# A macaron block on one core: from stages over both batch rows to one batch row beside the other's expert matmuls

## The chip, the cores and the metric

The kernel runs on one core of one Trainium2 chip, launched once. The metric is the device time of that core in microseconds (us); the median of three runs stands for a kernel. PE is TensorE, DVE VectorE, ACT ScalarE, POOL GpSimd, and SP the sync engine, which only issues DMAs here.

## The reference

`x` has 2 batch rows of 2048 tokens with 128 features, all in fp32. Three residual parts follow one another:

```python
x = x + 0.5 * ffn(layernorm(x))     # 4 experts, each token goes to one of them
x = x + attn(layernorm(x))          # linear attention with 32 features
x = x + 0.5 * ffn(layernorm(x))     # the same expert weights again

def ffn(x):                         # W1: 4 x 128 x 512, W2: 4 x 512 x 128
    idx = argmax(softmax(x @ Wg + bg))
    y = gelu(x @ W1 + b1) @ W2 + b2     # for every expert
    return y[idx]
def attn(x):
    q1, k1 = (elu(p) + 1 for p in (x @ Wq.T @ proj, x @ Wk.T @ proj))
    kv = k1.T @ (x @ Wv.T)              # summed over the 2048 tokens of a batch row
    return (q1 @ kv) / (sum(q1) + 1e-8)
```

Only the sum `kv` joins tokens, and only those of one batch row. Everything else is done for each token alone.

## The kernel before

The kernel works on both batch rows together, in stages that follow one another:

1. **Front.** `x` is loaded as 32 tiles of 128 tokens. DVE makes the layer norm, PE transposes and multiplies by `Wg`, and rows of `x` and of its norm are stored to a buffer in DRAM (`rows0`).
2. **Routing** (`route_dve`, `route_pe`). DVE finds each token's expert and, with two small matmuls, its place in an order by expert. Each expert gets whole tiles of its own, so 32 tiles become T1 = 35, with empty slots at an expert's end. A one-hot matrix `SL` and the table `AV` turn this into a list `src` of the rows of each tile.
3. **Experts** (`ffn_pool`, `ffn_pe`, `ffn_act`, `ffn_dve`), 35 tiles. POOL gathers a tile by an indirect DMA (L548); PE transposes it (L595), multiplies by W1 (`up`, L602) and, after ACT's GELU (L644), by W2 (`down`, L612). DVE copies the expert's W1 and bias into `w1e` (L666), adds residual and bias (L675) and the result of `down` (L686). The buffers `g_in`, `w1e`, `res` have U = 4 copies.
4. **Attention**, over all 35 tiles in groups of 5: `la_*` makes features and the sums, `lb_*` (L823, L832 to L844) the result and the statistics of the next layer norm. Two-row masks keep the batch rows apart. Rows go to `rows1`.
5. **Routing** again, 6. **Experts** again, now with a scatter of each tile to the output (L556), by the token number that the row carries.

Each engine runs a program of its own in the order in which its block is written, and waits on semaphores; `run_steps` and `run_groups` write loops with a peeled head and tail. Nothing is reordered at run time. So no matmul of an expert stage can be issued while PE's program stands in attention or routing. An fp32 matmul counts as two instructions in the profile, a transpose as one: a tile has 8 for `up`, 8 for `down` and 1 for the transpose.

Of the kernel before, what the change touches and what calls it, by code (L numbers as in the profile page):

```python
# [5 lines left out]
class Step:  # L15

    def __init__(self, j, k, turns16, bufs):
        self.j, self.k, self.turns16, self.bufs = j, k, turns16, bufs  # L20

    def plus(self, d):
        k = self.k + d
        return Step(self.j + d, k % self.bufs, self.turns16 + 16 * (k // self.bufs), self.bufs)

    def at_most(self, last):
        return not isinstance(self.j, int) or self.j <= last


def step_of(j, bufs):  # L30
    return Step(j, j % bufs, 16 * (j // bufs), bufs)


def run_steps(eng, head, loop_end, n, bufs, body, enter=None, after_loop=None):

    assert head % bufs == 0 and (loop_end - head) % bufs == 0
    shared = None
    for j in range(head):  # L40
        if enter and j % bufs == 0:
            shared = enter(j)
        body(step_of(j, bufs), shared)
    with eng.Fori(head, loop_end - bufs + 1, bufs) as i:
        shared = enter(i) if enter else None
        for u in range(bufs):
            body(Step(i + u, u, i * (16 // bufs), bufs), shared)
    if after_loop:
        after_loop()
    for j in range(loop_end, n):  # L50
        if enter and j % bufs == 0:
            shared = enter(j)
        body(step_of(j, bufs), shared)


def run_groups(eng, n, parts, before=None):


    most = max(lag for lag, _ in parts)
    loops = (n - 3) // 2  # L60

    def peeled(s):
        if before:
            before(s)
        for lag, body in parts:
            if 0 <= s - lag < n:
                body(step_of(s - lag, 2))
    for s in range(3):
        peeled(s)
    if before:  # L70
        before(3)
    with eng.Fori(3, 2 + 2 * loops, 2) as i:
        for u in range(2):

            st = Step(i + u, (1 + u) % 2, (i - 1) * 8 + 16 * ((1 + u) // 2), 2)
            for lag, body in parts:
                body(st.plus(-lag))
    for s in range(3 + 2 * loops, n + most):
        for lag, body in parts:
            if 0 <= s - lag < n:  # L80
                body(step_of(s - lag, 2))


class Stage:


    AHEAD = 2
# [8 lines left out]
def need(eng, stage, j):  # L96

    if isinstance(j, int) and j < 0:
        return
    eng.wait_ge(stage.sem, j + 1 + Stage.AHEAD)  # L100


def build(nc, x, wq, wk, wv, proj, w1, b1, w2, b2, wg, bg, out):
# [5 lines left out]
    TOKENS = B * L  # L109
# [3 lines left out]
    T0 = TOKENS // P  # L113
    T1 = T0 + NE - 1
    GS0, GS1 = 4, 5
    NG0, NG1 = T0 // GS0, T1 // GS1
    U = 4
    EW = F + NC
    WG = 96
    EPS_LN, EPS_Z = 1e-5, 1e-8  # L120
    FAR = 2 * TOKENS
    BANK = 512
    assert D == P and T1 % GS1 == 0 and T0 % GS0 == 0 and B == 2 and B * R <= P

    x_rows = x.rearrange("b l d -> (b l) d").rearrange("(p t) d -> p t d", t=T0)
    out_rows = out.rearrange("b l d -> (b l) d")


    RW0, RW1 = 2 * D, 2 * D + 1
    rows0 = nc.dram_tensor("rows0", (TOKENS, RW0), f32, kind="Internal").ap()  # L130
    rows1 = nc.dram_tensor("rows1", (P * T1 + 1, RW1), f32, kind="Internal").ap()
    rows0_v = rows0.rearrange("(p t) c -> p t c", t=T0)
    rows1_v = rows1[0:P * T1, :].rearrange("(p t) c -> p t c", t=T1)

    with ExitStack() as ctx:
# [3 lines left out]
        def pair(name, shape, dt=f32, n=2):  # L139
            return [sb(f"{name}{i}", shape, dt) for i in range(n)]  # L140
# [961 lines left out]
```

## Time and profile before

| | us |
|---|---|
| median of 3 runs | 353.05 |
| the runs | 349.28 to 356.53 |
| span of the profiled execution (no other time of it is given) | 349.7 |
| PE busy | 248.7 (71%) |
| DVE busy | 174.6 (50%) |
| POOL busy | 145.9 (42%) |
| ACT busy | 136.8 (39%) |

The span is the time from the first to the last instruction. "Busy" is the union of an engine's instructions; for PE it also holds time in which matmuls overlap. A stage is found in the trace by its lines: PE's first `up` starts at 56.15 us, its last instruction of the first expert stage ends near 128, routing lies around 205 to 223, the second expert stage from 228 to 338.

### The profile page before, as it was taken

To read this page: it belongs to the slowest core of one execution; us is meant where nothing else is said; L and a number is where in the kernel's file an instruction comes from. 1 tells how busy PE (TensorE), PEld (TensorE's weight loads), DVE (VectorE), ACT (ScalarE), POOL (GpSimd) and SP (SyncE) were. 2 spreads that over 40 slices of the span, in tenths; PEclk is the share of its full clock that TensorE was granted. 3 is DMA by queue.
4 is the path that set the end of the run, shared out by engine and by line. 5 is a ranking of instruction groups with operands and counts; after the bars stand their busy time and mean duration, and the time that the engine had idled before them with its cause. 6 is when DMAs were issued, how large, how long until landed. Compare 5 with 4: busy or idle time off the path is not lost. (4 is left out here: it accounts for less than half of the span.)

```text
span 349.7 us, 7231 instructions
## 1 busy us (share of the span) xinstructions
PE 248.7 (71%) x1825; PEld 232.3 (66%) x1826; DVE 174.6 (50%) x791; ACT 136.8 (39%) x436; POOL 145.9 (42%) x172
## 2 busy tenths in 40 slices
PE   0577036999999997997699640669687776876740
PEld 0566026999999996986599540659676765875740
DVE  3965882456555578836655249723232333233320
ACT  0133003666667634551644420036441543353520
POOL 2710216354454264220523202256557555765650
PEclk9999655999999999998555665599789889889995
DMA  6946503122222203222593400031212212212200
GB/s 248 301 126 195 148 2 90 50 73 69 66 60 62 59 2 148 83 72 74 153 184 100 114 0 0 13 95 55 61 54 68 60 53 60 68 53 60 51 26 0
DMA packets 27941, 28.45 MB, mean 81 GB/s; under 512 B 2938, under 2 KB 23052, under 8 KB 27666
## 3 DMA queue, kind: packets, MB, share of 16 engines
q1 hardware_dynamic: 20274, 14.57, 14.7%
q0 software_dynamic: 4480, 11.30, 11.6%
q10 hardware_dynamic: 3168, 2.36, 2.3%
q8 instruction: 8, 0.13, 0.1%
q14 instruction: 11, 0.09, 0.1%
HBM read 13.87 MB, written 11.09 MB: 71 GB/s over the span
## 5 line engine op out<-in xcount | busy, mean ns | idle before, releaser
L644 ACT ACTIVATE hT<-PA,w1e 128x128 f32<-128x128 f32 x280 | 80.0, 371 | 65.9 <-PE PA L602 32.3
L602 PE MATMUL PA<-hT_in,w1e 128*128 128x128 f32 x560 | 83.3, 296 | 21.6 <-DVE w1e L666 10.7
L548 POOL DMA_INDIRECT g_in<-rows,g_idx x70 | 68.6, 980 | 59.5 <-issue 21.2
L602 PEld LDWEIGHTS PA<-hT_in,w1e 128*128 128x128 f32 x560 | 75.2, 209 | 24.5 <-ACT hT_in L638 20.9
L612 PE MATMUL PC<-W,hT 128*128 x560 | 78.1, 286 | 0.2 <-issue 0.2
L612 PEld LDWEIGHTS PC<-W,hT 128*128 128x128 f32 x560 | 72.5, 203 | 0.4 <-issue 0.3
L556 POOL DMA_INDIRECT out_dram<-o_out,o_idx x35 | 36.6, 1046 | 33.1 <-issue 16.1
L638 ACT ACTIVATE hT_in<-PD 128x128 f32<-128x128 f32 x70 | 20.4, 292 | 64.6 <-PE PD L595 57.6
L685 DVE COPY o_idx<-token 128x1 int32<-128x1 int32 x35 | 5.3, 153 | 72.1 <-PE PC L612 50.1
L666 DVE COPY w1e<-W 128x516 f32 x72 | 29.9, 422 | 0.9 <-DVE W L974 0.8
L595 PE MATMUL PD<-ident,g_in 128*128 128x128 f32 x70 | 21.4, 306 | 11.1 <-DMA g_in<-rows,g_idx 10.7
L353 PE MATMUL PA<-ident,xn 128*128 128x128 f32 x102 | 19.1, 327 | 10.1 <-DVE xn L343 3.6
L686 DVE SCALAR_TENSOR_TENSOR X<-PC,res 128x128 f32 (+1 forms) x35 | 10.2, 292 | 30.3 <-PE PC L612 26.3
L366 PE MATMUL PB<-Wg,xnT 128*128 128x96 f32 x134 | 23.0, 337 | 0.0
L854 ACT ACTIVATE xn<-X,nmr,rstd 128x128 f32 (+1 forms) x35 | 14.2, 481 | 21.8 <-POOL nmr L816 21.0
L1003 PE MATMUL PB<-ident 128*128 128x128 f32 x72 | 13.0, 360 | 13.5 <-DVE STATS L957 12.2
L353 PEld LDWEIGHTS PA<-ident,xn 128*128 128x128 f32 x102 | 14.2, 173 | 12.6 <-issue 12.6
L366 PEld LDWEIGHTS PB<-Wg,xnT 128*128 128x128 f32 x134 | 22.4, 255 | 0.2 <-ACT xnT L360 0.2
L322 POOL TENSOR_TENSOR MR<-VE,neghalf 128x4 f32<-128x4 f32 (+1 forms) x15 | 16.0, 1108 | 14.3 <-DVE VE L313 14.2
L343 DVE TENSOR_SCALAR xn<-X,mr 128x128 f32 (+1 forms) x67 | 19.2, 350 | 5.2 <-DMA rows<-xn 2.1
L360 ACT ACTIVATE xnT<-PA 128x640 f32<-128x640 f32 (+1 forms) x22 | 14.5, 661 | 17.8 <-PE PA L353 17.8
L520 PE MATMUL PC<-AV,SL 128*128 128x70 bf16 x67 | 5.7, 249 | 21.9 <-DVE SL L464 21.9
(148 smaller groups left out, 286.5 us busy)
## 6 DMA issues: line engine op xcount, KB each, us to landing
rows<-X SPq DMA_DIRECT2D x7, 322.5 KB, 4.0
XN<-xn SPq DMA_DIRECT2D x7, 320.0 KB, 2.5
rows<-xn SPq DMA_DIRECT2D x7, 320.0 KB, 4.6
X<-in_L_attn_x_dram SPq DMA_DIRECT2D x2, 1024.0 KB, 6.5
rows<-xn SPq DMA_DIRECT2D x8, 256.0 KB, 2.3
rows<-X SPq DMA_DIRECT2D x1, 2048.0 KB, 9.5
g_in<-rows,g_idx POOLq DMA_INDIRECT x70
qs<-QT SPq DMA_DIRECT2D x7, 160.0 KB, 2.6
```

The costliest lines, as they stand in the source:

```text
L322: eng.tensor_tensor(MR[:, g * gs:(g + 1) * gs, 1], VE[:, g * gs:(g + 1) * gs], neghalf[:, 0:gs], ALU.pow)\
L343: i = eng.tensor_scalar(xn[k][:, t, :], row(X, st.j * gs + t), mr[k][:, t, 0:1], mr[k][:, t, 1:2], ALU.subtract, ALU.mult)
L353: i = eng.transpose(area[:, t * P:(t + 1) * P], xn[st.k][:, t, :], ident[:, :])
L366: i = eng.matmul(PB[:, BANK * st.k + t * WG:BANK * st.k + (t + 1) * WG], xnT[st.k][:, t * P:(t + 1) * P], Wg[:, :], start=True, stop=True)
L548: eng.indirect_dma_start(out=g_in[k][:, 0:RW], out_offset=None, in_=rows, in_offset=bass.IndirectOffsetOnAxis(ap=g_idx[k][:, 0:1], axis=0))\
L556: eng.indirect_dma_start(out=out_rows, out_offset=bass.IndirectOffsetOnAxis(ap=o_idx[k][:, 0:1], axis=0), in_=o_out[k][:, :], in_offset=No ...
L595: s["xT"].done(eng.transpose(bank(PD, st.k % 2, P), g_in[st.k][:, ln_at:ln_at + D], ident[:, :]))
L602: i = eng.matmul(PA[:, BANK * (st.k % 2) + c * P:BANK * (st.k % 2) + (c + 1) * P], w1e[st.k][:, c * P:(c + 1) * P], hT_in[st.k % 2][:, :], ...
L612: i = eng.matmul(bank(PC, st.k % 2, D), hT[st.k][:, c * P:(c + 1) * P], W2[:, bass.ds(e + c * P, D)], start=(c == 0), stop=(c == NC - 1))
L638: s["xTs"].done(eng.activation(hT_in[st.k % 2][:, :], bank(PD, st.k % 2, P), ACT.Copy))
L644: i = eng.activation(hT[st.k][:, c * P:(c + 1) * P], PA[:, BANK * (st.k % 2) + c * P:BANK * (st.k % 2) + (c + 1) * P], ACT.Gelu, bias=w1e[ ...
L666: s["w1e"].done(eng.tensor_copy(w1e[st.k][:, :], W1[:, bass.ds(e, EW)]))
```

## The change

The diff rewrites nearly all of `build`. Its parts:

- **Phases.** There are four expert phases: FFN 0 of batch row 0, FFN 0 of row 1, FFN 1 of row 0, FFN 1 of row 1. Attention and the second routing of row 0 are issued among the expert matmuls of phase 1, those of row 1 among phase 2; the first routing of row 1 among phase 0. A constant table of visit numbers places them. All loops are unrolled.
- **Dense sorting, masked visits.** A row's 2048 tokens are sorted by expert without gaps into T = 16 tiles. A tile that holds two experts is visited by both: V = T + 3 = 19 visits a phase, 76 in all against 70 tiles before. DVE multiplies bias and result of a visit by a 0/1 `mask` per token and adds them to the gathered row in place.
- **W1 slabs by DMA.** SP copies, for every visit, the expert's W1, b1 and b2 (128 x 644 fp32, 330 KB, SBUF to SBUF) into one of 5 `slab` buffers, issued 4 visits ahead. DVE's copy is gone. W2 is still read in place.
- **Gathers.** All 16 tiles of a phase have their own place in SBUF (`G0`, `G1`), so no gather waits for a buffer; a row is x, mean and 1/std (520 bytes), where it was x and its norm (1024). There are 64 gathers and 32 scatters (70 and 35 before).
- **Layer norm.** Gate and attention weights are centred once, so PE transposes raw rows; mean and 1/std are applied later.
- **Attention.** `K'X` is one 128x128 sum; the result is made 4 tiles at a time by one matmul with 512 columns on a block diagonal `KV`. Masks for two batch rows are gone.

```diff
-    T1 = T0 + NE - 1
-    U = 4
+    T = L // P
+    V = T + NE - 1
+    NSLAB, NXN, NHT = 5, 3, 3
+        LN_LEAD, TURN_LEAD, UP_LEAD, RES_LEAD, SLAB_LEAD = 4, 3, 2, 2, 4
 # SP
+            def copy_slab(s):
...
+                need(eng, ffn["hT"], s - NSLAB)
+                need(eng, ffn["res"], s - NSLAB)
+                eng.dma_start(slab[k][:, :], W1[:, bass.ds(offs[s], SW)]).then_inc(s_slab[k], 16)
+            for s in range(2 * B * V):
+                if s + SLAB_LEAD < 2 * B * V:
+                    copy_slab(s + SLAB_LEAD)
...
 # GpSimd
+            for v in range(V):
+                if v + 12 < T:
+                    gather(1, 0, v + 12)
+                if v == 0:
+                    pow_la(1, NG - 1)
+                if 5 <= v < 5 + NG:
+                    pow_lb(1, v - 5)
+                if v >= 13:
+                    gather(1, 1, 2 * (v - 13))
+                    gather(1, 1, 2 * (v - 13) + 1)
+                if v >= 4:
+                    scatter(0, v - 4)
 # DVE
-                s["w1e"].done(eng.tensor_copy(w1e[st.k][:, :], W1[:, bass.ds(e, EW)]))
+                ffn["res"].done(eng.scalar_tensor_tensor(out=r, in0=slab[s % NSLAB][:, F + NC:SW],
+                                                         scalar=mask[f][b][:, v:v + 1], in1=r, op0=ALU.mult, op1=ALU.add))
+                ffn["out"].done(eng.scalar_tensor_tensor(out=r, in0=DN[s % 2][:, 0:D], scalar=mask[f][b][:, v:v + 1],
+                                                         in1=r, op0=ALU.mult, op1=ALU.add))
+            for s in range(2 * B * V):
+                finish(s)
+                if (ahead := tile_ahead(ph, v, LN_LEAD)):
+                    norm(*ahead)
+                if s + RES_LEAD < 2 * B * V:
+                    residual(s + RES_LEAD)
+                if f == 0 and v >= NE:
+                    la_stat(b, v - NE)
...
+                if ph in (1, 2):
+                    if v == 2:
+                        la_features(o)
+                    if v == 3:
+                        la_gt(o)
+                    if v == 4:
+                        la_kv(o)
+                    if 5 <= v < 5 + NG:
+                        lb_x2(o, v - 5)
+                    if v == 10:
+                        route_hot(1, o)
+                    if v == 11:
+                        route_slots(1, o)
+                        route_hots(1, o)
+                    if v == 12:
+                        route_visits(1, o)
+                    if v == 13:
+                        route_src(1, o)
 # PE
+            def down(s):
+                need(eng, ffn["hT"], s)
+                need(eng, ffn["out"], s - 2)
...
+            for s in range(2 * B * V):
+                if (ahead := tile_ahead(ph, v, TURN_LEAD)):
+                    turn_in(*ahead)
+                if s + UP_LEAD < 2 * B * V:
+                    up(s + UP_LEAD)
+                down(s)
...
+                if ph in (1, 2):
+                    if v == 3:
+                        la_sum(o)
+                    if v == 4:
+                        la_kv(o)
+                    if 5 <= v < 5 + NG:
+                        lb_num(o, v - 5)
+                    if 6 <= v < 6 + NG:
+                        side_turn(o, v - 6, 1)
+                    if 7 <= v < 7 + NG:
+                        side_gate(o, v - 7)
+                    if v == 11:
+                        counts(ph + 1)
+                    if v == 13:
+                        inverse(ph + 1)
 # ACT
+                if ph in (1, 2):
+                    if v == 2:
+                        la_exp(o)
+                    if v == 3:
+                        la_q(o)
```

PE's program before, where the second attention part (L366 is its gate matmul) passes into routing (L512 to L520) and the second expert stage:

```order
L366 MATMUL PB<-Wg,xnT 128x96 x10
L512 MATMUL PC<-hot_b,ones_b 128x140
L513 MATMUL PC<-hot_b,below_b 128x140
L520 MATMUL PC<-AV,SL 128x70 x35
L1003 MATMUL PB<-ident 128x128 x10
L595 MATMUL PD<-ident,g_in 128x128 x2
L602 MATMUL PA<-hT_in,w1e 128x128 x4
```

PE's program of the change, at visit 3 of phase 1 (L759 is the end of that visit's `down`, L804 and L810 are `la_sum` of row 0, L741 and L751 the transpose and `up` of the next visits of row 1):

```order
L759 MATMUL DN<-W,hT 128x128
L804 MATMUL S<-KR,G_0 128x128 x16
L810 MATMUL S<-ident,KQ 128x128 x4
L741 MATMUL TR<-ident,xn 128x128
L751 ISA
L751 MATMUL U<-hT_in,slab 128x128 x4
```

The attention sum moved from a stage of its own to a place between two visits of the other row.

DVE's program before, in the second routing (nothing of an expert tile stands near it):

```order
L457 TENSOR_TENSOR AV<-tile_f,lane_f 128x35x35
L460 TENSOR_SCALAR AV<-AV,part 128x35x35
L464 TENSOR_TENSOR SL<-slot_b,lane_b 128x896 x5
L469 TENSOR_SCALAR ge<-lane_f,tstart 128x35 x3
L471 TENSOR_TENSOR gsum<-ge 128x35
```

DVE's program of the change, at the end of visit 11 of phase 1 (L465 to L474 end row 0's routing, L570 and L571 scale row 1's features; L550 is `finish` of visit 12, L538 `residual` of visit 14):

```order
L465 TENSOR_SCALAR slot_i<-pos_i 128x16
L466 TENSOR_TENSOR A<-tile_i,lane_f 128x256
L468 TENSOR_SCALAR AV<-A,part 128x16x16
L469 TENSOR_TENSOR AV<-A,lane_f 128x16x16
L474 TENSOR_TENSOR SL<-slot_i,lane_b 128x512 x4
L570 TENSOR_TENSOR KQ<-S,RS_1 128x4x2x32
L571 TENSOR_SCALAR KM<-KQ 128x2x128
L550 SCALAR_TENSOR_TENSOR G_1<-DN,mask_1,G_1 128x128
L538 ISA
L538 SCALAR_TENSOR_TENSOR G_1<-slab,mask_1,G_1 128x128
```

What moved: the routing of 16 tiles now stands in front of the `finish` that PE's `down` of visit 14 waits for.

POOL's program before, in the loop of the second expert stage (a gather and a scatter in turn):

```order
L548 DMA g_in<-rows,g_idx 128x257
L100 REGISTER_ALU
L556 DMA out_dram<-o_out,o_idx 4096x128
```

POOL's program of the change, at visits 8 to 14 of phase 2 (L304 is the last power of row 1's layer norm, L321 scatters row 0's result, L314 gathers row 1's tiles for phase 3):

```order
L304 TENSOR_TENSOR G_1<-VE_1,neghalf 128x4
L321 DMA out_dram<-G_0 4096x128 x5
L314 DMA G_1<-rows_1,src_1 128x131 x2
L321 DMA out_dram<-G_0 4096x128
L314 DMA G_1<-rows_1,src_1 128x131 x2
```

What moved: the gathers of phase 3 stand in pairs among the scatters of phase 2, and no buffer of a tile holds them back.

## Rows read from the trace of the kernel before

**Rows 1.** The page: the span, and the granted TensorE clock in 40 slices.
```profile
span 349.7 us, 7231 instructions
...
PEclk9999655999999999998555665599789889889995
```

**Rows 2.** Busy time by stretch: stretch, length, PE, PEld, DVE, ACT, POOL, then clock, DMA share, GB/s.
```profile
56.10:127.80 71.70, 71.38 (x605) 70.45 (x605) 39.12 (x179) 47.66 (x176) 32.81 (x35) 0.96 0.21 61
127.80:204.80 77.00, 65.76 (x413) 59.40 (x412) 42.63 (x186) 34.45 (x72) 23.73 (x40) 0.76 0.39 105
204.80:228.00 23.20, 7.69 (x57) 6.57 (x57) 19.08 (x54) 0.00 (x0) 4.85 (x4) 0.57 0.02 6
228.00:338.50 110.50, 82.75 (x596) 77.36 (x595) 34.42 (x207) 46.65 (x175) 67.66 (x68) 0.91 0.22 60
338.50:349.70 11.20, 0.00 (x0) 0.00 (x0) 0.00 (x0) 0.00 (x0) 0.81 (x1) 0.62 0.00 0
164.00:193.00 29.00, 25.89 (x112) 23.91 (x113) 17.65 (x94) 14.58 (x35) 11.06 (x24) 0.50 0.62 149
```

**Rows 3.** PE in order of time: start, length, instruction.
```profile
56.15 1.92 PE L602 MATMUL PA<-hT_in,w1e 128*128 128x128 f32 x8
...
85.54 0.27 PE L595 MATMUL PD<-ident,g_in 128*128 128x128 f32 x1
...
87.44 0.27 PE L595 MATMUL PD<-ident,g_in 128*128 128x128 f32 x1
```

**Rows 4.** POOL in order of time, second expert stage.
```profile
252.50 1.01 POOL L556 DMA_INDIRECT out_dram<-o_out,o_idx  x1 [0.30 <-issue]
...
255.10 1.01 POOL L556 DMA_INDIRECT out_dram<-o_out,o_idx  x1 [0.30 <-issue]
```

**Rows 5.** Waits from 230 to 338: who waited for what, us in total, times, longest.
```profile
ACT hT L644 <- remote: 23.0, 7, 4.7
```

**Rows 6.** DVE in order of time, front and first routing.
```profile
6.27 3.19 DVE L957 BATCH_NORM_STATS2 STATS<-X 128x6 f32<-128x128 f32 x16 [1.10 <-DMA X<-in_L_attn_x_dram]
...
36.19 0.17 DVE L432 TENSOR_SCALAR cnt_i<-cnt 128x4 int32<-128x4 f32 x1
36.40 0.17 DVE L433 TENSOR_SCALAR til_i<-cnt_i 128x4 int32<-128x4 int32 x1
...
49.63 0.18 DVE L480 TENSOR_SCALAR src<-rb 128x35 int32<-128x35 f32 x1
```

**Rows 7.** PE's gate matmuls of one group of four tiles, in order of time.
```profile
25.07 1.03 PE L366 MATMUL PB<-Wg,xnT 128*128 128x96 f32 x8
```

**Rows 8.** Groups by line and form: count, busy us, mean ns, idle time before.
```profile
L675 DVE TENSOR_TENSOR res<-g_in,B 128x128 f32<-128x128 f32 x70 | 19.8, 284 | 0.2 <-issue 0.2
...
L464 DVE TENSOR_TENSOR SL<-slot_b,lane_b 128x512 bf16<-128x512 bf16 x1 | 0.7, 678 | 0.0
```

**Rows 9.** DVE in order of time, second attention part, five tiles a line.
```profile
161.77 1.38 DVE L832 SCALAR_TENSOR_TENSOR X<-PC,Z,X 128x128 f32<-128x128 f32 x5 [1.63 <-PE PC L823]
...
164.89 1.35 DVE L832 SCALAR_TENSOR_TENSOR X<-PD,Z,X 128x128 f32<-128x128 f32 x5
```

**Rows 10.** ACT in order of time: the front's copies and a table load, then an expert tile.
```profile
30.90 0.60 ACT L360 ACTIVATE xnT<-PA 128x512 f32<-128x512 f32 x1 [1.13 <-PE PA L353]
31.52 1.28 ACT L1064 ACT_TABLE_LOAD   x1
...
86.75 1.14 ACT L644 ACTIVATE hT<-PA,w1e 128x128 f32<-128x128 f32 x4 [0.59 <-issue]
87.76 0.29 ACT L638 ACTIVATE hT_in<-PD 128x128 f32<-128x128 f32 x1
```

**Rows 11.** The page on DMA: queues (packets, MB, share of 16 engines), one issue (KB, us to landing).
```profile
q1 hardware_dynamic: 20274, 14.57, 14.7%
q0 software_dynamic: 4480, 11.30, 11.6%
...
XN<-xn SPq DMA_DIRECT2D x7, 320.0 KB, 2.5
```

More of the change, by code:

```diff
@@ new lines, in build @@
+        s_slab = [sem(f"s_slab{k}") for k in range(NSLAB)]
+        s_gather = [[sem(f"s_gather{b}_{t}") for t in range(T)] for b in range(B)]
+        s_scatter = sem("s_scatter")
+        s_dve = sem("s_dve")
+        ln0 = stages("ln0", "ve rstd")
+        fr = stages("fr", "xT xTs mm")
+        rt = stages("rt", "lgm hot cnt cb sl inv tab visit src")
+        ffn = stages("ffn", "norm xT xTs up hT down res out")
+        sd = stages("sd", "xT xTs mm")
+        la = stages("la", "ve rstd kq exp kr gt gts kv kvs qT qTs")
@@ L579, in experts_of, with tau, visit_ahead, loaded @@
+        def tau(ph, t):
+            return ph * T + t
+        def visit_ahead(s, lead):
+            return divmod(s + lead, V) if s + lead < 2 * B * V else None
+        def loaded(eng, table, ph, lo, n, top_value):
+            f, b = divmod(ph, 2)
             _, values = nc.values_load_multi_w_load_instructions(
-                expert[f][0:1, bass.ds(j, n)], engines=[eng.engine], min_val=0, max_val=(NE - 1) * EW,
-                skip_runtime_bounds_check_because="DVE sums at most NE-1 comparisons times EW")
@@ L847, in lb_norm @@
-        def lb_norm(eng, st):
-            k = st.k
-            need(eng, lb["nmr"], st.j)
-            xn_free(eng, lb, s_rows1n, st)
-            alone(eng)
-            for t in range(GS1):
-                i = eng.activation(xn[k][:, t, :], row(X1, st.j * GS1 + t), ACT.Identity,
-                                   bias=nmr[k][:, t:t + 1], scale=rstd[k][:, t:t + 1])
-            lb["xn"].done(i)
-        def ahead(eng, s, names):
-            for n in names.split():
-                for _ in range(Stage.AHEAD):
-                    eng.sem_inc(s[n].sem)
+                table[f][b][0:1, lo:lo + n], engines=[eng.engine], min_val=0, max_val=top_value,
@@ new lines, in _ @@
+            for k in range(NG, 2 * NG):
+                front_turn(k)
+                if k > NG:
+                    front_gate(k - 1)
+            front_gate(2 * NG - 1)
+            inverse(0)
+            eng.wait_ge(s_foldd, 5)
+            need(eng, rt["visit"], 0)
+            busy(12)
+            eng.wait_ge(s_w["w2"], 16 * NE)
+            eng.wait_ge(s_half, 2)
+            for t in range(TURN_LEAD):
+                turn_in(0, t)
+            for s in range(UP_LEAD):
+                up(s)
```

1464 lines of the change are left out of this document (680 added, 784 removed).

## The prediction, made before the changed kernel was run

> **What bounds the kernel now.** I read the granted clock and the span first [rows 1], then the busy time by stretch [rows 2], then PE, DVE, ACT and POOL in order of time. No one engine bounds the whole. In the first expert stage PE is the bound: 71.38 of 71.70 us busy at clock 0.96 [rows 2], one tile each 1.90 us [rows 3], the transposes at 85.54 and 87.44 being 17 instructions apart, so 0.112 us each. In the attention stretch (77 us) the clock is 0.76, and 0.50 in a part of it with PE nearly always busy [rows 2]. In the routing stretch (23.2 us) PE does 7.7 us of work and DVE 19.1 [rows 2]. The second expert stage does the same matmuls as the first and takes 110.5 us instead of 71.7, with PE busy 82.75 at 0.91 [rows 2]. There POOL issues a gather and a scatter per tile, one after the other: 2.60 us between two scatters [rows 4], and ACT waits 23.0 us in 7 long waits on something the trace only calls remote [rows 5]: gathers that came late, since a gather is held back until a buffer is free. So the reader is to see 350 us that hold about 70 tiles x 1.90 = 133 us of expert matmuls, and long stretches in which PE waits for other work. The change puts that other work among the matmuls.
>
> **The sum**, against the span of 349.7 us. The median of the runs, 353.05, is 3.4 us above it; I add 3 at the end.
>
> *Front, up to PE's first `up`* (56.15 before [rows 3]). The visits now start when row 0 alone is routed. Two pieces of x landed by 6.27 [rows 6]; a quarter comes a little sooner, and row 0's statistics are 16 x 0.2 = 3.2 us [rows 6] plus two times seven small operations, about 2: ready near 10.5. Centring the weights costs DVE 1.5. PE then needs four groups of a gate product, 1.03 us each [rows 7], plus transposes and copies of 0.60 [rows 10], at half clock at first: 6 us at full, 12 at half; I take gates done at 18. DVE: finding the expert, 7 operations, 2 us; half of row 1's statistics, 2.5; copies, 0.7; places, 10 small operations at 0.21 (36.19 to 36.40) [rows 6] and three of 256 elements, 3.9; four one-hots of 0.68 [rows 8], 2.6; the visit table, 11 small ones, 2.3; `src`, 0.7. That makes 32.7. From `src` to the first `up` it was 56.15 - 49.8 = 6.4 us before [rows 6, 3], and the gather, landing, transpose and copy are the same. Start: 39 us. Weights and stores are hidden: DMAs of megabytes end well before 32.
>
> *Expert matmuls.* 76 visits x 16 + 64 transposes = 1280 instructions x 0.112 = 143 us. Before, 35 tiles took 71.7 instead of 66.5 us [rows 2, 3], the start being at half clock: plus 5.
>
> *Side work on PE.* For each batch row: 32 transposes 4 us, four gate groups 3.6 to 4.1, four key/query groups (same shape) 3.6, the sum `K'X` 32 x 0.112 = 3.6, its query transposes and small products 0.8, and four products of 512 columns, each 2 x 4 x 0.112 = 0.9 (scaled by columns from [rows 3]), 3.6: 19.3. Two rows 38.6, and three routings among the visits, 1.6 each: 43 us.
>
> *Waits.* ACT needs 1.14 + 0.29 = 1.43 per tile [rows 10], DVE about 4 operations of 0.29 [rows 8], 1.15: both are under 1.90 in plain visits. Where DVE's side work is longer than the two visits that PE may run ahead (`down` needs `out` of two visits before), PE waits:
> - Routing at visits 10 to 13 is 11.5 us of DVE (the terms above) beside 4 x 1.15; the one-hots hold back `inverse` on PE by 2 us, then `finish` of 12 to 14, and the first norm of the next phase waits for a gather (issue 1.3, landing 2) behind `src`. I add that up to 8.4 us in phase 1, 7 in phase 2, 6 for the first routing of row 1 in phase 0.
> - `lb_x2`: four tiles are 4/5 of 3.12 = 2.5 us [rows 9], about 2.9 with waits, plus 1.15; PE has 1.9 + 0.9 + 0.5 + 1.0 = 4.3 there. Nearly even: 2 us a phase, 4.
> - Features: DVE's last key group comes 1 us late for `la_sum`: 2 in all. ACT's exp costs four table switches of 1.28 [rows 10]; they lie beside `la_sum` and cost nothing. If `la_sum` were not there, they would cost 2.6 us a batch row.
> - POOL at visits 13 to 18 of phase 2 has two gathers and a scatter, 3 x 1.30 = 3.9 us [rows 4] per visit of 1.9: phase 3 starts 3 us late.
> - Handoffs: 3. Sum of waits: 33 us.
>
> The table load began 0.02 us after ACT's last copy ended [rows 10]. The Trainium skill (ScalarE: Activation LUTs, What ACT_TABLE_LOAD costs) adds to each switch a drain of 1.38 us; the trace does not show one in front of the load. By the page the exp of each batch row would come late by about 1.4 us more, and the sum would be 3 us higher.
>
> *Clock.* PE idles of some 3 us precede half clock now and then: 0.91 over the second expert stage [rows 2], 10 of 110 us. With some six such waits here I take 10 us. The trace cannot show it; the ends are 0 (first expert stage after its start) and the rival below.
>
> *W1 slabs.* 330 KB each. The nearest row is a copy of the same kind, 320 KB in 2.5 us from issue to landing [rows 11], with 3 visits (5.7 us) of lead. Their load: queue 1 moved 14.57 MB in 14.7% of the span, 283 GB/s [rows 11], so 1.16 us a slab; 105 indirect DMAs took 11.6%, 0.39 us each: 1.55 of 1.90 us a visit. I take zero for it; ends 0 and the rival of a bound by DMA. Removed: DVE's copy, which was hidden in the first stage.
>
> *Tail*: 13.4 us from PE's last instruction (336.3) to the end, of which the last 11.2 hold one scatter [rows 2]. Unchanged.
>
> Sum: 39 + 143 + 5 + 43 + 33 + 10 + 13 = 286; with 3, **about 290 us**.
>
> **The rivals.**
> 1. *The overlap is better than I count* (chance 0.18). The waits that I added are partly the same time, and nothing drops the clock: waits 15, clock 0, start 36. That is 286 - 18 - 10 - 3 + 3 = 258. For it: DVE's work in phases 1 and 2 sums to 58 and 48 us, PE's to 55 and 51, so with looser order they would fit; against: the order within each engine is fixed, and visit 12's `finish` stands behind the routing.
> 2. *DMA becomes the pace* (0.15). Near the ends of phases 1 and 2 two gathers, a scatter and a slab are 1.16 + 3 x 0.39 = 2.3 us a visit, above 1.90. If each slab needed the 2.5 us of [rows 11] in turn, all visits would take 2.5: 76 x 0.6 = 46 more, minus waits then covered (some 12): 324. Against: landings contain a fixed part that overlaps. By the Trainium skill (DMA: Bandwidth & Descriptors, Issuing engines are not separate DMA queues) slabs from SP and gathers from POOL share the same 16 engines, so moving them to another queue does not help.
> 3. *PE runs at half clock through phases 1 and 2* (0.08): the other side. For it: in 164 to 193 the same kinds of work, with DVE and PE handing groups to and fro, ran at 0.50 although PE was busy 25.9 of 29.0 us [rows 2]. PE has about 55 + 51 = 106 us of work there; at half clock that is 106 more, minus the 10 already counted and 12 of waits that it covers: 290 + 84 = 374, slower than before. It decides from about 63 us more on, which is half clock over three quarters of the two phases. Against: expert matmuls stand between all side work, and the first expert stage held 0.96. The Trainium skill (TensorE: Matmul & The Clock Gate, HAM oscillation) says that waits between bursts bring the clock down again and again; the trace agrees with 0.91 in the second expert stage.
> 4. *The change does not overlap as it says* (0.04): a wait that stands far ahead in one engine's program (row 1's first routing, `store_rows1` in SP's queue ahead of slabs, or the unrolled program's own loading) stops all, phases 1 and 2 then take their side work one after the other: DVE's 37 and 32 us of it beside PE's 19 each, some 60 more: 350, no change.
>
> **How the numbers follow.** The forecast has 0.55, with 275 to 305 as its own range: 290, with waits between 20 and 45 and the clock between 3 and 15. The predicted time is 290. The range of 8 in 10 reaches down to rival 1 and up to rival 2: 257 to 325; outside lie rivals 3 and 4 and some of the tails. A median that differs by 2%, 7 us, can be told from no change (three runs spread over 7.3 us). Faster: forecast, rivals 1 and 2: 0.88; within 2%: rival 4, 0.04; slower: 0.08.
>
> **What would show it.** Right: PE's first `up` near 39 us; visits of phase 3 at 1.9 to 2.0 us; PE busy above 80% between the first `up` and the last; PE waits of 3 us and more at visits 12 to 16 of phases 1 and 2, released by DVE's one-hots or by the norm of a tile just gathered; phases of about 51, 70, 67 and 38 us. Slab waits on PE near zero. Wrong: PE waiting on slabs (rival 2), clock 0.5 over most of phases 1 and 2 (rival 3), a start after 45 us, or a single wait of over 10 us (rival 4).

## The result, and the profile after

| | kernel before | changed kernel |
|---|---|---|
| median, us (4 runs each, on one chip) | 354.79 | 385.38 |
| runs, us | 349.28 to 361.11 | 384.32 to 388.27 |
| span of the profiled execution, us | 349.7 | 386.5 |

The changed kernel is **slower: 1.096 times the time before, 95% interval 1.084 to 1.108**. A ratio with an interval compares only each kernel's runs within 1.5% of its fastest, so it can differ a little from the quotient of the medians beside it. The forecast was 290, its range ended at 325, and slower had a chance of 0.08.

The page of the changed kernel answers [rows 1] and [rows 11] (TensorE's busy share, the granted clock in slices, the queues with packets, MB and share of 16 engines):

```profile
span 386.5 us, 6148 instructions
...
PE 260.2 (67%) x1764; PEld 238.0 (62%) x1764; DVE 159.7 (41%) x663; ACT 130.1 (34%) x410; POOL 118.6 (31%) x134
...
PEclk9988685598999978989988598989886559698995
...
q1 hardware_dynamic: 20928, 31.44, 23.5%
```

PE is busy 67% of a longer span, and no engine is near full, nor the DMA engines. The phases, as [rows 2] has the stages of before (stretch, length, PE, PEld, DVE, ACT, POOL, clock, DMA share, GB/s); the first `up` was at 44.72 us:

```profile
44.70:128.30 83.60, 57.91 (x390) 53.70 (x390) 31.62 (x128) 29.73 (x103) 25.87 (x27) 0.81 0.31 99
128.30:218.70 90.40, 66.74 (x480) 60.57 (x480) 47.41 (x202) 34.93 (x107) 24.54 (x25) 0.87 0.26 95
218.70:314.00 95.30, 66.37 (x444) 60.47 (x444) 41.35 (x168) 33.17 (x104) 35.70 (x36) 0.80 0.28 100
314.00:374.90 60.90, 44.43 (x301) 40.58 (x301) 16.25 (x50) 22.99 (x81) 17.64 (x19) 0.88 0.25 90
```

The forecast had 51, 70, 67 and 38 us. The last phase holds nearly plain visits, so it is the place to look. PE there, in order of time, answers [rows 3] (a number in brackets is the idle time before, with what ended it):

```profile
345.44 0.33 PE L741 MATMUL TR<-ident,xn 128*128 128x128 f32 x1 [0.70 <-DVE xn L524]
348.77 1.66 PE L751 MATMUL U<-hT_in,slab 128*128 x8 [3.00 <-issue]
...
355.78 0.33 PE L741 MATMUL TR<-ident,xn 128*128 128x128 f32 x1 [0.70 <-DVE xn L524]
355.98 1.15 PE L751 MATMUL U<-hT_in,slab 128*128 x8
356.96 1.06 PE L759 MATMUL DN<-W,hT 128*128 x8
358.72 0.33 PE L741 MATMUL TR<-ident,xn 128*128 128x128 f32 x1 [0.70 <-DVE xn L524]
```

And DVE at the same visits:

```profile
358.06 0.35 DVE L550 SCALAR_TENSOR_TENSOR G<-DN,mask,G 128x128 f32 x1 [1.99 <-PE DN L759]
358.33 0.34 DVE L524 TENSOR_SCALAR xn<-G 128x128 f32<-128x128 f32 x1
```

The times in the brackets of these eight lines point at two faults.

**Fault A: a ring through two engines.** From transpose to transpose it is 2.94 us (355.78 to 358.72), not the 1.90 of [rows 3]. `down` ends, DVE does `finish` (L550, 358.06) and only behind it the norm (L524, 358.33) of the tile four visits ahead, and PE's next transpose (358.72) wants that norm. PE and DVE take turns, though the norm needs nothing that `down` or `finish` makes.

**Fault B: register loads on PE.** Once in five visits PE stands 3.00 us on "issue", with no engine named. Its two register loads stand there (name, count, shortest/median/longest in ns, first and last start). The same view of the kernel before follows in the second fence:

```profile
L209 PEldq TENSOR_LOAD <-v_w x16: 584/1235/1546, 43.0 to 362.5; - x16
L209 PEldq TENSOR_LOAD <-v_in x16: 585/1430/2189, 43.9 to 364.1; - x16
```

```profile
L579 PEldq TENSOR_LOAD <-expert x18: 329/334/782, 57.2 to 331.3; - x18
```

Before, one load of 334 ns for four tiles; now two of 1235 and 1430 (medians) for five visits.

**The late ends.** A third loss answers [rows 5]. The waits of the changed kernel (who waited for what, us in total, times, longest):

```profile
PE TR L741 <- DVE xn L524: 49.9, 39, 10.4
DVE G L550 <- remote: 42.7, 5, 14.7
PE U L751 <- issue: 29.6, 15, 3.0
ACT hT L929 <- remote: 17.8, 4, 9.6
```

The longest wait of each of the two remote rows lies at one place. Here are PE, ACT, DVE and POOL around it, each in order of time:

```profile
295.44 2.07 PE L751 MATMUL U<-hT_in,slab 128*128 x8 [1.15 <-issue]
297.31 1.91 PE L759 MATMUL DN<-W,hT 128*128 x8
...
304.58 1.14 ACT L929 ACTIVATE hT<-U,slab 128x128 f32<-128x128 f32 x4 [9.60 <-remote]
...
308.93 0.35 DVE L550 SCALAR_TENSOR_TENSOR G<-DN,mask,G 128x128 f32 x1 [14.74 <-remote]
...
294.87 1.00 POOL L321 DMA_INDIRECT out_dram<-G  x1 [0.30 <-issue]
296.18 0.97 POOL L314 DMA_INDIRECT G<-rows,src  x1 [0.30 <-issue]
```

By the records, PE's `up` ended at 297.5 and its `down` at 299.2. ACT needs only that `up`, and starts at 304.58; DVE needs only that `down`, and starts at 308.93. So PE's results were taken up 7 and 10 us later than its records end: only one core runs, so "remote" is no other core here, but a wait whose release the profile can't place. I call this a late end; whether the matmuls or their semaphores are late, the records don't show. POOL issues indirect DMAs without a pause meanwhile, 0.30 us apart, 17 in a row from 284.6 to 306.1 us. The kernel before has such waits in its second expert stage: that is what [rows 5] shows, which I had read as gathers that came late. There 5 to 8 indirect DMAs follow one another without a pause. In the same trace the first expert stage, where behind the first six at most three gathers do, has no remote wait at all.

### The profile page after: what moved, and what is told of

Read it like the earlier page. It is cut to its first block and busy times, and to the rows that moved or that the text cites. A ratio compares the mean times of both kernels' runs of the same rounds, so it can differ in the third digit from the quotient of the medians.

```text
span 386.5 us, 6148 instructions
## 1 busy us (share of the span) xinstructions
PE 260.2 (67%) x1764; PEld 238.0 (62%) x1764; DVE 159.7 (41%) x663; ACT 130.1 (34%) x410; POOL 118.6 (31%) x134
## 3 DMA queue, kind: packets, MB, share of 16 engines
q1 hardware_dynamic: 20928, 31.44, 23.5%
## 5 line engine op out<-in xcount | busy, mean ns | idle before, releaser
L929 ACT ACTIVATE hT<-U,slab 128x128 f32<-128x128 f32 x304 | 86.6, 368 | 112.3 <-PE U L751 87.4
L751 PE MATMUL U<-hT_in,slab 128*128 x608 | 101.6, 319 | 30.8 <-issue 29.6
L751 PEld LDWEIGHTS U<-hT_in,slab 128*128 128x128 f32 x608 | 88.3, 224 | 35.9 <-issue 34.1
L759 PE MATMUL DN<-W,hT 128*128 x608 | 95.5, 310 | 0.1
L550 DVE SCALAR_TENSOR_TENSOR G<-DN,mask,G 128x128 f32 x76 | 26.7, 351 | 163.7 <-PE DN L759 115.9
L759 PEld LDWEIGHTS DN<-W,hT 128*128 128x128 f32 x608 | 89.5, 226 | 0.3 <-issue 0.3
L314 POOL DMA_INDIRECT G<-rows,src x64 | 61.9, 967 | 62.5 <-DVE src L510 44.7
L741 PE MATMUL TR<-ident,xn 128*128 128x128 f32 x64 | 22.4, 350 | 65.1 <-DVE xn L524 49.9
L741 PEld LDWEIGHTS TR<-ident,xn 128*128 128x128 f32 x64 | 9.9, 154 | 76.1 <-DVE xn L524 58.6
L321 POOL DMA_INDIRECT out_dram<-G x32 | 31.5, 984 | 61.5 <-DVE G L550 57.7
L538 DVE SCALAR_TENSOR_TENSOR G<-slab,mask,G 128x128 f32 x76 | 27.6, 363 | 16.4 <-DVE xn L524 6.7
L524 DVE TENSOR_SCALAR xn<-G 128x128 f32<-128x128 f32 x64 | 22.1, 346 | 7.2 <-DMA G<-rows,src 5.6
L304 POOL TENSOR_TENSOR G<-VE,neghalf 128x4 f32<-128x4 f32 x8 | 8.2, 1028 | 52.1 <-DVE VE L612 52.1
L938 ACT ACTIVATE xTs<-S 128x512 f32<-128x512 f32 x16 | 9.6, 600 | 14.2 <-PE S L773 11.9
```

The costliest lines, as they stand in the source:

```text
L314: eng.indirect_dma_start(out=row(f, b, t, 0, RW), out_offset=None, in_=(rows0, rows1)[f][b], in_offset=bass.IndirectOffsetOnAxis(ap=src[f] ...
L321: eng.indirect_dma_start(out=out_rows, out_offset=bass.IndirectOffsetOnAxis(ap=index, axis=0), in_=row(1, b, t), in_offset=None).then_inc( ...
L524: ffn["norm"].done(eng.tensor_scalar(xn[k % NXN][:, :], row(f, b, t), row(f, b, t, D, 1), row(f, b, t, D + 1, 1), ALU.subtract, ALU.mult))
L538: ffn["res"].done(eng.scalar_tensor_tensor(out=r, in0=slab[s % NSLAB][:, F + NC:SW], scalar=mask[f][b][:, v:v + 1], in1=r, op0=ALU.mult, o ...
L550: ffn["out"].done(eng.scalar_tensor_tensor(out=r, in0=DN[s % 2][:, 0:D], scalar=mask[f][b][:, v:v + 1], in1=r, op0=ALU.mult, op1=ALU.add))
L741: ffn["xT"].done(eng.transpose(TR[:, 0:P], xn[k % NXN][:, :], ident[:, :]))
```

## The experiments

Each time is a median on one chip, beside the kernel before on the same chip. The 18 runs came in five batches, each on one chip, and the batches fell into two kinds: in three of them the kernel before took 349 to 355 us (as in the result), in two 329 to 331. I call them kind L and kind S. Times are compared within a kind only. For e8 to e10 there is no interval: of the seven runs of the kernel before in their batch one took 347.9 us and six 354.1 to 357.1, and against the 347.9 the three ratios would be 0.926, 0.982 and 0.944.

| run | kind | us | before | ratio (95% interval) |
|---|---|---|---|---|
| e0, changed kernel again | L | 383.6 | 353.5 | 1.083 (1.067 to 1.099) |
| e15, changed kernel a third time | L | 381.6 | 349.1 | 1.096 (1.083 to 1.108) |
| e1, norm ahead of finish | S | 305.2 | 330.7 | 0.922 (0.919 to 0.925) |
| e2, loads of four values | S | 308.0 | 330.7 | 0.930 (0.926 to 0.934) |
| e3, both | S | 276.3 | 330.7 | 0.835 (0.831 to 0.839) |
| e11, both again | S | 276.6 | 329.3 | 0.853 (0.844 to 0.861) |
| e8, both again | L | 322.2 | 354.7 | 0.908, of medians |
| e4, changed kernel, gathers apart | S | 368.6 | 330.7 | 1.117 (1.111 to 1.123) |
| e5, four values, one column off | L | 392.8 | 353.5 | 1.102 (1.089 to 1.114) |
| e6, norm first, eight values | L | 319.5 | 353.5 | 0.905 (0.898 to 0.913) |
| e7, both, weights issued by SP | L | 315.7 | 353.5 | 0.894 (0.886 to 0.901) |
| e9, both, gathers apart | L | 341.8 | 354.7 | 0.964, of medians |
| e10, both, scatters later | L | 328.6 | 354.7 | 0.927, of medians |
| e12, e9 with POOL kept busy | S | 355.8 | 329.3 | 1.097 (1.093 to 1.101) |
| e13, both, gathers paced | S | 274.2 | 329.3 | 0.846 (0.840 to 0.852) |
| e14, e13, weights issued by SP | S | 272.9 | 329.3 | **0.842 (0.840 to 0.845)** |
| e16, e14 again | L | 302.1 | 349.1 | **0.869 (0.859 to 0.878)** |

### Fault A: e1

```
-                finish(s)
                 if (ahead := tile_ahead(ph, v, LN_LEAD)):
                     norm(*ahead)
+                finish(s)
```

> VectorE does norm(s+4) ahead of finish(s); nothing else differs from the changed kernel. Theory A (each transpose stands behind the norm, the norm behind the finish of the down just done): plain visits fall from 2.95 us to 1.9-2.1 us, TensorE's wait at L741 on xn falls from 49.9 us to under 20 us, the time from 385 to 325-350. Rival B (the five-value register loads set the pace): the pitch between loads falls too but the load stalls of about 2.8 us stay, so 355-370. Rival C (only the bursts of gathers matter): under 5 us gained, 380-386. Rival D (TensorE's half clock is what makes visits slow): visits stay at 2.5 us or more.

305.2 us, a ratio of 0.922. The expected times were reckoned from 385 us, a kind L time; as ratios, theory A's 325 to 350 are 0.92 to 0.99, and the run is at their low end, far from the others. That is a rough comparison, since the changed kernel was never timed in kind S; the waits say more. The waits of PE, and PE in plain visits of the last phase:

```profile
PE U L751 <- issue: 25.8, 12, 3.3
...
PE TR L741 <- DVE xn L524: 10.7, 7, 4.1
```

```profile
264.28 0.27 PE L741 MATMUL TR<-ident,xn 128*128 128x128 f32 x1
264.39 1.06 PE L751 MATMUL U<-hT_in,slab 128*128 x8
265.28 1.06 PE L759 MATMUL DN<-W,hT 128*128 x8
266.17 0.27 PE L741 MATMUL TR<-ident,xn 128*128 128x128 f32 x1
```

The pitch is 1.89 us and the wait for the norm 10.7 instead of 49.9: fault A is shown. Rival D falls, since the visits are at full pace. The load stalls stayed (25.8).

### Fault B: e2, e5, e6

`e2` is `-    CHUNK = 5` / `+    CHUNK = 4`, nothing else.

> Register loads of four values each instead of five (20 chunks instead of 16, on TensorE, VectorE and SyncE). Theory B: TensorE's loads fall from 1.2-1.4 us to about 0.35 us each as in the kernel before, the idle at L751 'issue' from 29.6 us to under 10, and the time by 15-30 us, to 355-370. If the loads are slow for another reason (TensorE's sequencer waits on the DVE's write of the table, or on memory) they stay at 1.2 us and, with four more chunks, the time rises by 3-6 us.

```profile
L209 DVEq TENSOR_LOAD <-v_row x20: 340/344/1259, 42.3 to 289.6; - x20
L209 PEldq TENSOR_LOAD <-v_w x20: 327/334/1110, 42.4 to 285.3; - x20
L209 PEldq TENSOR_LOAD <-v_in x20: 328/332/773, 43.0 to 286.5; - x20
```

308.0 us, well below the 355 to 370 expected, a range that again goes by kind L (what the loads cost in kind S is read from e1 and e3 below). The loads fell to a quarter, and PE's idle on issue at L751 went from 29.6 to 2.7 us. But why does a fifth value cost 900 ns? In the changed kernel the shortest PE loads take 585 ns from column 0 of a table, 1235 from columns 5 and 10, and about 1000 for the four values from column 15. So not the fifth value but the start may count. `e5` has loads of four, each one column later:

```
-        ... [several(f"{n}{f}_", [P, V], B, i32) ...
+        ... [several(f"{n}{f}_", [P, V + 1], B, i32) ...
-                table[f][b][0:1, lo:lo + n], ...
+                table[f][b][0:1, 1 + lo:1 + lo + n], ...
-   did(eng.tensor_scalar(v_slab[f][b][:, :], ...       (and the other three tables)
+   did(eng.tensor_scalar(v_slab[f][b][:, 1:V + 1], ...
```

> Loads of four values each, as in e2_chunk4, but every table begins one column later, so that no load starts at a multiple of four values. In the changed kernel's trace a TensorE load of five values takes 585 ns from column 0, 1235 ns from columns 5 and 10, and a load of four values from column 15 about 1000 ns; in e2_chunk4 four values from columns 0, 4, 8, 12 take 332 ns. Theory B1 (a start off a multiple of four values is what costs, some 245 ns a value): loads of 1000 ns here and a time 20-30 us above e2_chunk4, 325-340 us. Theory B2 (the fifth value is what costs): loads stay at 332 ns, 306-312 us.

```profile
L209 DVEq TENSOR_LOAD <-v_row x20: 740/964/1400, 43.6 to 375.9; - x20
L209 PEldq TENSOR_LOAD <-v_w x20: 764/1000/1185, 43.3 to 371.6; - x20
```

The same four values take 1000 ns instead of 334. In time, e5 stands beside e0, the changed kernel in the same batch: 392.8 us against 383.6, with intervals of ratio that overlap, so nothing is left of what the shorter loads gain. `e6` is e1 with `CHUNK = 8`:

> Norm ahead of finish, and loads of eight values from columns 0, 8 and 16. Theory B1 (start on a multiple of four values is enough): about 0.4-0.7 us a load, 12 loads of a table instead of 20, the time within 3 us of e3_both's 276. Theory B2 (more than four values cost): 1.3-2 us a load, 285-300 us.

```profile
L209 DVEq TENSOR_LOAD <-v_row x12: 594/607/1445, 42.4 to 297.3; - x12
L209 PEldq TENSOR_LOAD <-v_w x12: 593/782/1217, 42.4 to 293.0; - x12
```

Eight values from columns 0 and 8 take about 595 ns at the shortest, and so in seven of DVE's eight such loads; on PE more than half take longer, up to 1217. Those from 16, three values left, take 780. So, by the shortest loads: **four values whose start is a multiple of four cost some 330 ns, four more behind them 260; a value left over behind them, and every value of a load that starts elsewhere, costs about 250 by itself** (5 x 248 = 1240; 4 x 250 = 1000; 330 + 250 = 580 for five from column 0; three left over 780). The start counts, not the fours inside: in the kernel before, DVE loads five values from columns 3, 7 and so on, with a whole four inside each, and takes 1183 ns. B1 is shown, B2 falls. Both runs were in a batch of kind L, so their times can't be held against e2's and e3's 308 and 276; e6's 319.5 us is near e8's 322.2. The Trainium skill (Runtime: NRT & Kernel Launch, Instruction fetch mechanics) gives, for the register loads ahead of a kernel, some 200 ns a register even in bulk. The loads here, from tables in SBUF, come near that from a misplaced start (250 a register), and are below it from a good one (334 for four, 84 a register).

### Both: e3, e8, e11

> Norm ahead of finish and loads of four values together. If A and B are separate, the gains add: 300-330. If one hides the other, the time is that of the better of the two. What is left should be the stalls in bursts of gathers (about 35-45 us in all by theory C), the phase edges and the front.

276.3 us, below the expected range. From e1, fault B is worth 28.9 us (305.2 to 276.3); from e2, fault A 31.7 (308.0 to 276.3); together 60.6. The same shows in kind L inside one batch: e0, with both faults, took 383.6 us, and e6, with both out, 319.5, which is 64.1 less and 0.905 of the time before. The phases of e3:

```profile
44.40:98.50 54.10, 48.37 (x395) 46.31 (x396) 33.24 (x128) 29.13 (x104) 25.04 (x26) 0.93 0.45 145
98.50:165.10 66.60, 60.50 (x483) 56.23 (x482) 48.13 (x202) 34.68 (x108) 21.95 (x23) 0.95 0.35 126
165.10:225.30 60.20, 55.39 (x446) 50.65 (x446) 42.13 (x167) 33.01 (x105) 28.93 (x30) 0.97 0.43 151
225.30:261.30 36.00, 34.78 (x298) 33.47 (x296) 16.29 (x50) 21.66 (x81) 27.33 (x29) 1.00 0.53 181
```

Forecast were 51, 70, 67 and 38; PE is busy 199.03 of 216.90 us, 92%. The late ends, though, which I had expected to remain, were gone, in e3 as in e1, e2 and e4: no wait called remote in any. So I ran the changed kernel itself again, and e3 twice more.

> The changed kernel itself, on the chip of this batch. Its first run had stalls called remote (VectorE 42.7 us, ScalarE 17.8 us); none of the four kernels run since had any, and the kernel before took 330.7 us beside them instead of 354.8. If the stalls belong to that first chip or its moment (theory E): none here, 355-370 us, ratio to before 1.07-1.12. If they belong to the changed kernel's order and vanish with each of the edits (theory C): they are here again at the same visits, 380-388 us, ratio 1.15-1.18.

> e3_both again on this batch's chip. If the kernel before takes 350-355 us here, this kernel has late ends of matmuls at its gather bursts (phase starts 0, 2 and 3) and takes 312-322 us, a ratio of 0.89-0.91; if the kernel before takes 330 us, 276 us and 0.835.

> e3_both once more, as the base for the other three on this batch's chip. 315-323 us (ratio 0.89-0.91) where the kernel before takes 350-355, 276 us (0.835) where it takes 330.

e0 was of kind L and had its late ends at the same visits (ACT 8.68 us before 297.88), 383.6 us. e8 was of kind L too: 322.2 us, with these waits:

```profile
DVE G L550 <- remote: 41.9, 6, 13.0
ACT hT_in L923 <- remote: 26.0, 6, 8.8
```

e11 was of kind S: 276.6 and no such wait. One and the same kernel takes 276 us on one kind and 322 on the other. So the late ends did not vanish by my edits, as theory C had it: they come with the machine or its moment. The kernel before is longer in kind L too, hence 1.083 for e0 and not theory C's 1.15. Theory E, in the form that they belonged to the first chip alone, was wrong as well.

> The kernel before, on the chip of this batch, for its profile. Theory E (on some chips TensorE's matmuls end late while GpSimd issues indirect DMAs back to back, on others never): a run of 349-358 us has late ends of 2-6 us in its second expert layer, where gathers and scatters alternate without a pause; a run of about 330 us has none.

The kernel before ran at 348.2 us in the profiled execution in its batch, of kind L, and showed them:

```profile
DVE o_idx L685 <- remote: 40.6, 9, 4.6
ACT hT L644 <- remote: 17.4, 4, 5.0
```

Between the kinds lie 46 us for the kernel with both faults out (276 to 322) and about 22 for the kernel before (330 to 352). I put both down to the late ends; e16 below shows only that a part of the 46 goes when the gathers are paced. The kernel before was never profiled in kind S; that it has no late ends there is inferred from its time.

### The late ends and the gathers: e4, e9, e12, e13, e16

```
+                if t:
+                    eng.wait_ge(s_gather[b][t - 1], 16 * (f + 1))
                 RW = (RW0, RW1)[f]
```

> The changed kernel with each gather issued only once the gather ahead of it has landed, so that they come every 2.5-3.5 us instead of every 1.28 us. Theory C (indirect DMAs issued back to back hold up TensorE's matmuls): the stalls called remote on VectorE (42.7 us) and ScalarE (17.8 us) fall below 15 us together; the phase edges wait longer for rows, so the time is 360-385. Rival (instruction fetch, or the slab copies): the stalls of 8-14 us stay at the same visits (first visits of phase 0, of phase 2 and of phase 3), and the time rises by 10-25 us from the later rows.

368.6 us, but in kind S, where nothing was to be seen. The same edit on e8, `e9`, was of kind L:

> e8_both_again with each gather issued only when the one ahead has landed. Theory E (back to back issues are what holds TensorE up where the chip does that): on a chip with the late ends they fall below 8 us together and the time comes below e8_both_again by 10-25 us; on a chip without, it is slower than e8 by 5-15 us, because the rows of the next phase come later. Rival (the landing data, not the issues, or something that has no part in the gathers): the late ends stay, and it is slower than e8 on either chip.

```profile
56.81 1.01 POOL L316 DMA_INDIRECT G<-rows,src  x1 [1.78 <-DMA G<-rows,src]
```

```profile
PE TR L743 <- DVE xn L526: 50.9, 18, 17.0
...
DVE G L552 <- remote: 13.7, 4, 8.9
...
ACT hT L931 <- remote: 7.4, 2, 6.2
ACT hT_in L925 <- remote: 6.8, 2, 3.8
```

The remote waits on L550 (here L552) and on ACT fell from 41.9 and 34.0 to 13.7 and 14.2 us, not to below 8 together as expected. None is left before 243 us, where e8 had eleven (DVE's before 60.52 the longest, 12.52). Those that remain near the end (ACT's 2.99 and 6.24 us before 310.37 and 316.89, DVE's 8.88 before 319.06) are where nine scatters still follow each other without a pause, which the edit left as they were (305.85 to 316.09). The one at 246.92 also stands behind scatters without a pause (three from 242.01 to 245.53). So in kind L the late ends come with unbroken rows of POOL's indirect DMAs and go where these are kept apart; whether it is the DMAs or the unbroken work is the question of e12. In kind S nothing comes of it: e3 issues 39 in a row (215 to 265 us) without one late end. The time of e9 rose all the same, to 341.8: one gather per 2.8 us is too slow, and PE waits 50.9 us for the norms of late rows. The expected gain of 10 to 25 us was wrong for that reason.

`e12` is e9 with 1.65 us of other POOL work behind each gather:

```
+                o = (ph_of(f, b) * T + t) * 8
+                eng.tensor_tensor(fill[:, o:o + 8], mean_w[:, 0:8], neghalf[:, 0:8], ALU.pow)
```

> e9_both_spaced with a power of 128x8 on GpSimd (1.65 us, result unused) behind each gather's issue, so that GpSimd is busy nearly all the time while its gathers stay 3 us apart. Theory E1 (the indirect DMAs issued back to back are the cause): at the starts of phases 0 and 1 no late ends, as in e9; time within 5 us of e9's ratio to the kernel before, 0.964. Theory E2 (any unbroken work of GpSimd is): late ends of 5 us and more come back at the start of phase 0, and the time rises by 10 us or more.

It was of kind S: 355.8 us, no late ends, and PE waited 65.7 us for norms. It settles nothing between E1 and E2. One stretch of the kernel before bears on them: from 125.21 us on POOL does seven powers in 8.04 us without a pause, as long as a row of six indirect DMAs, and PE works beside them (7.92 of 9.10 us). No wait there is remote, in either of its two traces of kind L. That speaks for E1, the DMAs, but it is one stretch of each trace and no experiment.

`e13` issues the gathers of phases 0 to 2 once a visit:

```
             for t in range(4, 8):
+                need(eng, ffn["norm"], t - 5)
                 gather(0, 0, t)
...
+                    need(eng, ffn["norm"], v + 3)
                     gather(0, 0, v + 8)
...
+                    need(eng, ffn["out"], v - 2)
                     gather(0, 1, v - 8)
...                  (left out: phase 1's last wait for out of V + v - 2; of row 0's second layer three
                      gathers stand at v == 13, then one a visit, behind out of the visit before)
```

> e11_both_again with the gathers of phases 0 to 2 issued one a visit (gather t of phase 0 once the norm of tile t-5 is done, those of phase 1 and 2 each behind a finish) instead of in bursts; phase 3 as it was. Theory E: on a chip with late ends those of 8-10 us at the start of phase 0, 2-3 us at 111 and 124 us and 6 us at the start of phase 2 go, phase 3's 11-13 us stay: 300-312 us against 315-323. On a chip without them: within 3 us of 276.

> e13_paced with the issues of W1, W2 and b2 on SyncE, as in e7_front: 3-5 us below e13_paced, since ScalarE's first copy no longer waits for them.

> e14_paced_front beside it. On a chip with late ends: theory E gives 295-308 us (ratio 0.83-0.87), those left in phase 3; if pacing does not prevent them, 312-322 us as e7 and e8. On a chip without: 273 us, ratio 0.84.

e13: 274.2, e14: 272.9 in kind S; pacing costs nothing there, and e14's gain of 1.3 us on e13 is under the 3 to 5 expected. In kind L, e16: **302.1 us**, ratio 0.869 (0.859 to 0.878), inside the 295 to 308 of theory E, where e7, the same kernel without the pacing, had 315.7 us and 0.894 (0.886 to 0.901). Its phases 0 and 2, in the columns of e3's:

```profile
40.90:105.70 64.80, 51.26 (x390) 48.97 (x390) 33.41 (x130) 28.96 (x103) 27.74 (x28) 0.89 0.38 122
...
173.30:250.50 77.20, 56.68 (x439) 51.59 (x438) 42.58 (x166) 33.31 (x107) 39.56 (x40) 0.90 0.37 125
```

Phase 1 took 67.6. By the times of the last `finish`, e8's three were 73.0, 73.1 and 80.2. Phase 2 stays long: the gathers and scatters at its end were not paced, 17 follow each other from 224.9 to 246.4 us, and ACT waits 9.59 us there before 247.58. Late ends are left in phase 0 too (ACT's 4.09 us before 51.04), which took 64.8 where e3, in kind S, had 54.1.

### The front, and the scatters: e7, e10, e15

`e7` is e3 with the issues of W1, W2 and b2 moved from ACT's queue into SP's, behind those of x.

> Norm ahead of finish, loads of four values, and the issues of W1, W2 and b2 moved from ScalarE to SyncE, behind the loads of x. ScalarE's first copy then starts at about 8-9 us instead of 14.3, TensorE's wait of 7.2 us at L702 goes, and the first up comes 5 us earlier: 270-272 us against 276 for e3_both. If the front is bound by the arrival of x, the gathers or W1's slab copies instead, the time stays at 275-277.

ACT's first copy of the front, first of e3, then of e7:

```profile
14.28 1.09 ACT L918 ACTIVATE xTs<-U 128x512 f32<-128x512 f32 x2 [8.11 <-issue]
```

```profile
6.38 0.60 ACT L921 ACTIVATE xTs<-U 128x512 f32<-128x512 f32 x1 [0.22 <-PE U L703]
```

The first `up` came at 40.95 us instead of 44.4 in e3 and 43.3 in e8, so 2 to 3 us earlier and not 5. The forecast of 270 to 272 us was for kind S, and the run was of kind L: 315.7 beside e6's 319.5 in its batch, but e6 loads eight values at a time, and their intervals of ratio touch.

> e8_both_again with the last seven scatters of phase 2 issued in phase 3, behind the gathers of phase 3, so that the burst of gathers is not shared with them. The rows of phase 3 come 5-9 us earlier, the wait at its edge shrinks by 2-5 us; the end is bound by the same 48 indirect DMAs, so 0 to -5 us in all. Theory E: on a chip with late ends their sum stays about the same, since the issues stay back to back.

A miss: 328.6 against e8's 322.2. Without a pause the DMAs came in both (18 in a row here, 17 in e8), but DVE's late end at that edge is 15.69 us before 271.20, where e8 had 12.97 before 268.55, and ACT's are 8.24 and 7.37 us (before 262.73 and 271.24), where e8 had 3.79 and 3.87.

> The changed kernel a third time, beside the next one. On a chip where the kernel before takes 323-331 us the late ends should be absent and the time 350-365 us, a ratio of 1.07-1.10 (e4, which adds waits for rows, was at 1.117 there); on one where it takes 350-355 us, 380-388 us and 1.08-1.10 again. If the changed kernel's loss hangs on the late ends, its ratio on the first kind is 1.00-1.04.

Kind L again: 381.6 us, ratio 1.096. The changed kernel was thus never timed in kind S. If the two faults added there, it would take 305.2 + 308.0 - 276.3 = 337 us, 1.02 of the 330.7; e4, with waits of its own on top, took 1.117. Whether the change is slower there, or only no faster, stays open.

## Why the prediction was wrong

- **The step that failed** is in the waits: "ACT needs 1.14 + 0.29 = 1.43 per tile [rows 10], DVE about 4 operations of 0.29 [rows 8], 1.15: both are under 1.90 in plain visits." Throughput was compared, not order. DVE has time enough, but its norm stands behind `finish`, and so behind `down`; the ring of `down`, `finish`, norm and transpose took 2.94 us instead of 1.90. The handoffs, counted at 3 us in all, cost 31.7 (e2 to e3). The order of DVE's loop shows it without a trace.
- **A term that was missing**: the register loads, two on PE in each five visits. The sum gives them nothing, since before one load of 334 ns was hidden. They cost 28.9 us (e1 to e3). The trace of before had the clue, DVE's loads of 1183 ns in the same view, five values from a column off the fours.
- **A row read wrongly**: the 23.0 us of [rows 5] were put down to late gathers. They are ACT waiting for PE's `up` (L644), late ends beside unbroken indirect DMAs. The change makes longer rows of them, 13 to 17 at its three longest against 5 to 8; in kind L the kernel with both faults out is 46 us longer than in kind S, the kernel before some 22.
- *Front*: 39 forecast, 44.7 measured. The issues of the weights held ACT until 14.3 us, which I had costed at nothing because the DMAs themselves were hidden. With them moved it was 40.9.
- *Clock*: 10 us were added. In e3 it is 0.93, 0.95, 0.97, 1.00, better than that; in the changed kernel it is 0.80 to 0.88. Its longest idles of PE, 9.17, 7.95 and 10.37 us, are each followed by a stretch at half clock (0.50 from 59.8 to 64.8, from 214.4 to 219.0 and from 309.6 to 314.0). Rival 3 did not happen: it had half clock through phases 1 and 2, and they had 0.87 and 0.80.
- *Right*: that the side work hides among the visits (phases of 54, 67, 60, 36 against 51, 70, 67, 38 once the faults are out, in kind S), and that the W1 slabs cost nothing (no wait for one anywhere; 31.44 MB in 23.5% of the span, so rival 2 is out). PE's share was to be above 80%: it is 92% in e3, but 71% in the changed kernel, so there that sign said wrong.
- *Rivals*: slower came, though by none of them. Rival 3 named the side and not the cause. A count of what each engine's order waits for would have given a rival of 31.7 + 28.9 us on top of 290: 351, no change. That agrees with the 337 (1.02) worked out above for kind S; for the rest of the way to 1.08 to 1.10 in kind L only the late ends are known, and their share is not measured.

So 290 us described the program with its two faults out: 276 in one kind of batch, 316 to 322 in the other (302 with the gathers paced). That 290 lies between them is luck, for the late ends were not in the sum. As it was, the change lost 60 us to the two faults. In ratios of kind L: 1.083 to 1.096 with both, 0.89 to 0.93 without, so the faults decide between slower and faster there, late ends or not.

## What to carry to other kernels

When two engines work in step, compare not only their work per step but the order within it: an operation for a later tile that stands behind one for the present tile closes a ring, and its length is the pitch. Put the operation that looks ahead first. Count register loads as instructions of the engine that does them, in fours that start at a multiple of four. A wait called remote on one core was here a result of the core's own PE that came late: look at what else was being issued then, and run the kernel before and after on more than one chip before it goes into a sum.

## What the runs showed of the hardware

- A register load on TensorE of four int32 values takes 334 ns from a column that is a multiple of four, and 1000 ns from one that is not (medians of e2 and e5); eight from column 0 or 8 take 595 at the shortest and up to 1217 (e6). Four on VectorE take 344 and 964, on SyncE 298 and 1304.
- The same programs run 7% (kernel before, 330 and 352 us) and 17% (e3, 276 and 322 us) apart in two kinds of batch, and all of the late ends that were seen are in the longer. Two batches, one of each kind, carry the same chip number; whether that is one chip at two moments or two machines is not known. Nor is it shown whether the issue of indirect DMAs or any unbroken work of GpSimd delays TensorE's matmuls or their semaphores; only that the late ends at the gathers went when the gathers were kept apart (e9), and those at unbroken scatters stayed.
